# An output layernorm with a known mean: the rows of W2 and b2 centred once, z's squares summed on ScalarE

## What is computed

```python
x = x + gnn(layernorm(x))
#   h_neigh = segment_sum(h[src], dst) / deg
#   h = normalize(relu(h @ W_self[l] + h_neigh @ W_neigh[l] + b[l])),  l = 0, 1, 2
xn = layer_norm(layernorm(x), ln_g, ln_b)
top_p, top_i = top_k(softmax(xn @ Wg), 2);  conf = top_p / sum(top_p)
h = gelu(xn @ W1 + b1)                      # 8 experts x 64
combined = sum of conf * (h_e @ W2[e] + b2[e]) over the two experts
x = x + layer_norm(layernorm(x) + combined, out_g, out_b)
```

## Time and profile before

| what | value |
|---|---|
| median of three runs | 2080.27 us |
| the profiled execution | 2078.15 us, span 2076.4 us |
| granted TensorE clock over the span | 0.991 |
| TensorE busy | 1957.9 us (94%) |
| VectorE busy | 1627.2 us (78%) |
| ScalarE busy | 1034.4 us (50%) |
| GpSimd busy | 1225.1 us (59%) |

### The profile page before, as it was taken

How to read it: one execution, slowest core, us unless ns; L and a number is a source line. 1 busy time by engine, 2 the same in 40 slices (tenths; PEclk the granted TensorE clock), 3 DMA queues, 4 the chain that set the end, 5 groups by cost and what they waited for, 6 DMA issues and landing times.

```text
span 2076.4 us, 41132 instructions
## 1 busy us (share of the span) xinstructions
PE 1957.9 (94%) x13965; PEld 1064.1 (51%) x13965; DVE 1627.2 (78%) x3951; ACT 1034.4 (50%) x1877; POOL 1225.1 (59%) x1239
## 2 busy tenths in 40 slices
PE   6999999997999999999999999999899999999996
PEld 2444444443444444444444444444467767677774
DVE  7677986665777777776777777775689999999985
ACT  4444333332334434343344444553677777777762
POOL 2785116674656665664444444454568888888854
PEclk9999999998999999999999999999999999999998
DMA  6877678974787878874788886555878888878863
GB/s 209 205 184 230 238 253 151 142 136 119 189 192 202 193 196 188 202 187 147 207 236 233 235 233 191 175 172 165 224 171 180 183 186 186 182 179 181 185 99 50
DMA packets 330680, 384.93 MB, mean 185 GB/s; under 512 B 200057, under 2 KB 200231, under 8 KB 330471
## 3 DMA queue, kind: packets, MB, share of 16 engines
q1 hardware_dynamic: 269655, 216.86, 43.1%
q0 software_dynamic: 60816, 165.43, 31.1%
HBM read 175.81 MB, written 165.31 MB: 164 GB/s over the span
## 4 chain that ended last, share of the span: by engine, by line
PE 41%; DVE 25%; issue 12%; ACT 9%; DMA 8%; POOL 4%; SPq 0%; DVEq 0%; ACTq 0%; POOLq 0%
PE psY L578 18%; PE psS L578 18%; DMA w_n<-HH 6%; DVE R L1485 4%; ACT RR L1013 2%; POOL node_info L769 2%; DVE w_s L1693 2%; DVE area L1473 2%; DVE HH L1509 2%; DVE area L1683 2%; DVE st6b L1670 2%; PE psT L1798 2%; DVE w_s L1658 2%; DVE HH L1590 2%; DVE G L1473 1%
## 5 line engine op out<-in xcount | busy, mean ns | idle before, releaser
L578 PE MATMUL psY<-w_n,HT 128*128 128x512 f16 x1620 | 378.8, 384 | 21.8 <-DVE HT L1357 12.7
L578 PE MATMUL psS<-w_s,HT 128*128 128x512 f16 x1620 | 371.7, 379 | 0.0
L1013 ACT ACTIVATE RR<-R 128x512 f32<-128x512 f32 x237 | 149.6, 631 | 312.8 <-DVE R L1485 312.7
L878 POOL DMA_INDIRECT y_rows<-YB,poutT x158 | 160.8, 1018 | 198.0 <-DVE YB L1364 161.6
L578 PEld LDWEIGHTS psY<-w_n,HT 128*128 128x128 f16 x1620 | 157.5, 99 | 224.5 <-DVE HT L1357 23.9
L578 PEld LDWEIGHTS psS<-w_s,HT 128*128 128x128 f16 x1620 | 154.4, 98 | 167.8
L1374 DVE SCALAR_TENSOR_TENSOR SB<-psS,downs,bias 128x512 f32<-128x512 f32 x237 | 177.6, 749 | 76.6 <-PE psS L578 74.5
L578 PE MATMUL psY<-w_n 128*128 128x512 f16 x960 | 220.5, 379 | 12.4 <-DMA w_n<-HH 12.2
L578 PE MATMUL psS<-w_s,w_n 128*128 128x512 f16 x960 | 220.3, 379 | 0.0
L578 PE MATMUL psS<-w_w,w_s 128*128 128x512 f16 x948 | 217.5, 379 | 0.8 <-ACT w_s L1108 0.8
L1364 DVE SCALAR_TENSOR_TENSOR YB<-psY,YB 128x512 f16<-128x512 f32 x237 | 162.4, 685 | 47.8 <-ACT YB L980 47.6
(11 more groups left out here) (328 smaller groups left out, 3895.9 us busy)
## 6 DMA issues: line engine op xcount, KB each, us to landing
self_rows<-SB SPq DMA_DIRECT2D x236, 256.0 KB, 2.5
Sl<-self_rows SPq DMA_DIRECT2D x158, 256.0 KB
area<-in_x_dram SPq DMA_DIRECT2D x78, 256.0 KB, 5.1
y_rows<-YB SPq DMA_DIRECT2D x78, 256.0 KB, 5.1
out_dram<-obb SPq DMA_DIRECT2D x78, 256.0 KB
raw<-in_L_gnn_W_neigh_dram SPq DMA_DIRECT2D x12, 256.0 KB, 3.6
raw<-in_L_gnn_W_self_dram SPq DMA_DIRECT2D x12, 256.0 KB, 4.2
y_rows<-YB,poutT POOLq DMA_INDIRECT x158
```

The costliest lines, as they stand in the source:

```text
L578: mm = eng.matmul(acc, lhs[:, a, c, :], w[:, bpart, c, :], start=(c == 0 and n == 0), stop=(stop and c == KC - 1 and n == 2))
L878: pool.indirect_dma_start(Yd[l][:, :], bass.IndirectOffsetOnAxis(ap=poutT[:, t.t:t.t + 1], axis=0), YB[i][:, :], None, bounds_check=node_l ...
L1013: act.activation(RR[i][:, :], R[i][:, :], ACT.Relu).then_inc(s.rr, 1)
```

## The change

The rows of W2 (one per expert and hidden unit) and of b2 are centred: each row's mean is taken off. Then combined has mean 0 in every row, and z's mean is that of the residual part, a constant in the kernel's scale, `small[:, 7:8]`. z_gain subtracts this constant and waits for down alone. ScalarE sums the squares of z less the constant (z_squares), VectorE adds epsilon to one column (z_var), GpSimd takes the power as before. bn_stats and bn_aggr of z are gone. w2's steps move two later (WSTEP 24) and three jobs are new ahead of them.

```diff
 def WSTEP(m):
...
-    return 2 + 4 * (m - N_FIRST) + (m == 6)
+    return 2 + 4 * (m - N_FIRST) + (m >= 6) + (m == 7)
...
-            run_tiles(T, [(7, gather), (5, by_node), (4, norm3), (3, pow_of_group), (-10, zr_of),
-                          (-11, put_out)], 2)
+            run_tiles(T, [(7, gather), (-11, zr_of), (5, by_node), (4, norm3), (3, pow_of_group), (-11, put_out)], 2)
...
+                if name == "w2":
+                    act.wait_ge(s_wcent, 2)
                 after(act, s_cn, m)
                 act.activation(sqw, raw[:, m % 2, :, :], ACT.Square).then_inc(s_sq, 1)
...
-            def z_eps(t):
...
-                act.wait_ge(f3.aggz, (t + 1).n)
-                after(act, f3.zr, (t + -1).n)
-                act.activation(zv[:, i:i + 1], zm[:, i, 1:2], ACT.Identity, bias=ezb[:, t.group % 4, t.place:t.place + 1]
-                               ).then_inc(f3.zv, 1)
+            def z_squares(t):
...
+                act.wait_ge(f3.o1, (t + 1).n)
+                after(act, f3.zv, (t + -1).n)
+                act.activation(junk[:, :], psO[i][:, :], ACT.Square, bias=zshift[:, 0:1], scale=D ** -0.5,
+                               accum_out=zq[:, i:i + 1]).then_inc(f3.zq, 1)
...
+            def center_bias2():
+                rows = 6 * EXPERTS
+                dve.wait_ge(s_bload, 16 * 15)
+                link(dve.tensor_reduce(small[0:rows, 12:13], b2r[:, :], AX.X, ALU.add))
+                link(dve.tensor_scalar(small[0:rows, 12:13], small[0:rows, 12:13], -1.0 / D, None, ALU.mult))
+                dve.tensor_scalar(b2r[:, :], b2r[:, :], small[0:rows, 12:13], None, ALU.add).then_inc(s_wcent, 1)
+            def row_means():
+                m = C["w2"]
+                dve.wait_ge(s_wload[m % 2], 64 * (m // 2 + 1))
+                link(dve.tensor_reduce(small[:, 8:12], raw[:, m % 2, :, :], AX.X, ALU.add))
+                link(dve.tensor_scalar(small[:, 8:12], small[:, 8:12], -1.0 / D, None, ALU.mult))
+            def center_rows():
+                w = raw[:, C["w2"] % 2, :, :]
+                for c in range(KC):
+                    k = dve.tensor_scalar(w[:, c, :], w[:, c, :], small[:, 8 + c:9 + c], None, ALU.add)
+                k.then_inc(s_wcent, 1)
...
+                link(dve.tensor_scalar(zshift[:, :], small[:, 7:8], -(D ** -0.5), None, ALU.mult))
...
+                        (WSTEP(C["w2"]) - 3, center_bias2, None), (WSTEP(C["w2"]) - 2, row_means, None),
+                        (WSTEP(C["w2"]) - 1, center_rows, None),
...
-            def z_stats(t):
...
-                dve.bn_stats(st6b[:, :], psO[t.slot(2)][:, :]).then_inc(f3.bnz, 1)
-            def z_mean_var(t):
...
-                dve.bn_aggr(zm[:, t.slot(2), :], st6b[:, :]).then_inc(f3.aggz, 1)
+            def z_var(t):
...
+                dve.wait_ge(f3.zq, (t + 1).n)
+                after(dve, f3.zr, (t + -1).n)
+                dve.tensor_tensor(zv[:, i:i + 1], zq[:, i:i + 1], ezb[:, t.group % 4, t.place:t.place + 1], ALU.add
+                                  ).then_inc(f3.zv, 1)
             def z_gain(t):
...
-                dve.wait_ge(f3.aggz, (t + 1).n)
-                dve.scalar_tensor_tensor(Z[i], psO[i][:, :], zm[:, i, 0:1], ogb[:, :], ALU.subtract, ALU.mult
+                dve.wait_ge(f3.down, (t + 1).n)
+                dve.scalar_tensor_tensor(Z[i], psO[i][:, :], small[:, 7:8], ogb[:, :], ALU.subtract, ALU.mult
                                          ).then_inc(f3.o1, 1)
...
-            run_plan(T, [(-9, hs), (-5, confidences), (4, lambda t: carry_lo(t, 3)), (4, lambda t: combine(t, 3)), (3,
-                          x2), (-4, logits), (-9, flo), (4, norm_floor), (2, group_scales), (-4, largest), (-4, largest_index), (-4, gaps), (3, group_vars), (-10, z_stats), (-4, hots),
-                          (-10, z_mean_var), (-11, result), (-10, z_gain), (-1, xlo)],
+            run_plan(T, [(-9, hs), (-11, z_var), (-5, confidences), (4, lambda t: carry_lo(t, 3)), (4, lambda t: combine(t, 3)), (3,
+                          x2), (-4, logits), (-9, flo), (4, norm_floor), (2, group_scales), (-4, largest), (-4, largest_index), (-4, gaps), (3, group_vars), (-4, hots),
+                          (-11, result), (-10, z_gain), (-1, xlo)],
...
             def down(t):
...
-                after(pe, f3.o1, (t + -1).n)
+                after(pe, f3.zq, (t + -1).n)
```

More of the change, by code:

```diff
@@ L280, in __init__ @@
         self.down = sem("f3_down")
-        self.bnz = sem("f3_bnz")
-        self.aggz = sem("f3_aggz")
+        self.zq = sem("f3_zq")
         self.zv = sem("f3_zv")
@@ L419, in build @@
         s_wgain = sem("s_wgain")
+        s_wcent = sem("s_wcent")
         s_epad = sem("s_epad")
@@ L564, in build @@
         zv = sb("zv", [P, 2])
-        zm = sb("zm", [P, 2, 2])
-        st6b = sb("st6b", [P, 6])
+        zq = sb("zq", [P, 2])
+        zshift = sb("zshift", [P, 1])
         psA3 = [psA[0][:, :], psT[0].rearrange("p a c n -> p (a c n)").bitcast(F32)]
@@ L1110, in _ @@
             run_tiles(T, [(4, lambda t: carry_hi(t, 3)), (-9, fhi), (4, lambda t: relu(t, 3)), (4, sum_squares3), (-8,
-                          weights_in), (3, x2_deviations), (-1, xn), (-1, xhi), (-10, z_eps), (-4, gate_tanh), (-4, gelu)], 2)
+                          weights_in), (3, x2_deviations), (-1, xn), (-1, xhi), (-10, z_squares), (-4, gate_tanh), (-4, gelu)], 2)
         @block.vector
@@ L1665, in flo @@
                 dve.tensor_tensor(FH[i][:, 1, :], HS[i], FH[i][:, 0, :], ALU.subtract).then_inc(f3.flo, 1)
-            def z_stats(t):
+            def z_var(t):
                 t = t.own
-                dve.wait_ge(f3.down, (t + 1).n)
-                dve.bn_stats(st6b[:, :], psO[t.slot(2)][:, :]).then_inc(f3.bnz, 1)
-            def z_mean_var(t):
-                t = t.own
-                dve.wait_ge(f3.bnz, (t + 1).n)
-                after(dve, f3.zv, (t + -1).n)
-                dve.bn_aggr(zm[:, t.slot(2), :], st6b[:, :]).then_inc(f3.aggz, 1)
+                i = t.slot(2)
+                dve.wait_ge(f3.zq, (t + 1).n)
+                after(dve, f3.zr, (t + -1).n)
+                dve.tensor_tensor(zv[:, i:i + 1], zq[:, i:i + 1], ezb[:, t.group % 4, t.place:t.place + 1], ALU.add
+                                  ).then_inc(f3.zv, 1)
             def z_gain(t):
```

## The result

The changed kernel takes 2091.8 us (median of six runs, 2088.79 to 2096.39) beside 2077.74 for the kernel before (six runs): ratio 1.0076, interval 1.0059 to 1.0092. It is slower by 0.8%; forecast was 2075.5 us, between 2062 and 2086. It came out where the rival "GpSimd sets the pace" had put it (2091 us, chance 0.10); how far that was luck is said behind the experiments. The profiled execution took 2094.96 us (span 2093.2).

A forecast was written before the change was run, and what follows sets the result against it. The prediction took VectorE to bound the kernel's layer-3 part, at 28.99 us per four steps. From 2078.15 us it took 5.9 (steady part) and 1.5 (drain) and added 4.8 (first stage): 2075.5 us, range 2062 to 2086.

The forecast's parts named there:

- GpSimd sets the pace: Rival, layer 3 steady part: result waits for zr if GpSimd is late; 7.40 a step gives 2091 us; chance 0.10.
- GpSimd's order: Layer 3: zr_of moves from the step's end to behind the gather; costed at nothing, covered by GpSimd's slack.
- passes with two SBUF inputs stay four a step: Layer 3 steady part: argument against the GpSimd rival; result, x2, xlo and flo remain the contending VectorE passes.
- VectorE is rid of 0.73 a step: Layer 3 steady part: 0.83 us goes, z_var adds 0.10; VectorE's sum falls from 28.99 to 26.1 per four steps.
- The square costs 0.70 on the loop: Layer 3, ScalarE, combine to combine: 28.61 against 28.99 us per four steps, -5.9 us in all.
- What is late next: Layer 3 steady part: the next limit is ScalarE's chain, at 7.15 us a step, not TensorE.
- The drain: Last steps, without layer-3 tiles: 0.3 us saved in each of five steps, -1.5 us; ends 0 and -3.5.
- The first stage costs 4.8: First stage, w2: +2.54 row_means, +1.3 square sums, -1.35 wait gone, +2.34 weight_lo; ends 0 and +6.2.
- The sum: Whole kernel: 2078.15 - 5.9 - 1.5 + 4.8 = 2075.5 us.

The follow-up runs named there:

- The blocks: Five kernels, each run once: the kernel before plus a block behind its last step, GpSimd powers and gathers beside different VectorE work; no kernel time given.
- f3: Changed kernel with the power for zr ahead of the gather in GpSimd's order; 2074.76 us, ratio 0.9996 to the kernel before.
- f1: Changed kernel with result and put_out one step later, GpSimd's order kept; 2075.83 us, ratio 0.9989 to the kernel before.
- f2: f1 with the power for zr moved to the end of GpSimd's step; 2075.44 us, ratio 1.0006 to the kernel before.
- f6: Changed kernel with square ahead of relu and z_gain, z_var behind norm_floor, zr at GpSimd's step end, result one step later; 2063.45 us, ratio 0.9939.
- s1: Kernel before with only the centring and the shifted first-stage steps, z's statistics kept; 2081.89 us, ratio 1.0029.
- s2: Changed kernel without centring and with w2's steps where they were before; 2085.05 us, ratio 1.0034 to the kernel before.
- s3: Kernel before with only w2's first-stage steps later, nothing centred; 2079.22 us beside 2074.55, ratio 1.0021.

## Why the prediction was wrong

**The step that failed** is "GpSimd's order", the term for zr_of's move: "I cost the move at nothing; the cover is GpSimd's slack". The place where zr is made has no cover. The rows that would have said so are not among those of the prediction: GpSimd's timeline of the kernel before, here in the third step.

```profile
1809.29 2.12 POOL L922 DMA_INDIRECT out_dram<-w_s,poutT  x1 [0.18 <-issue]
1811.72 1.77 POOL L846 DMA_INDIRECT G<-y_rows,srcT  x1 [0.31 <-issue]
...
1815.71 0.54 POOL L913 TENSOR_TENSOR zr<-zv,halfpow 128x1 f32<-128x1 f32 x1
```

The gather ends at 1813.49, 2.43 after combine (1811.06), and so it does in the second and the fourth step (1806.23 and 1820.10). A power of 0.54 behind it ends 3.0 after combine. VectorE reaches result's place 3.20 and 3.26 after combine in the first two steps, but 2.60 and 2.67 in the third and fourth: against these places the power is 0.3 us early in the second step, and 0.4 and 0.3 late in the third and fourth. The prediction wanted the gather and the power done in the 3.2 us behind z_var, but gave neither a price and left put_out, here 2.12, out of them. In the changed kernel result waits for zr in the fourth and the second step, which are longer than forecast by 0.67 and 0.52; in the third its gather starts ahead of combine (1825.55, 1.05 long) and the power is just in time. The move also put a power under x2 and flo, out of a place at the step's end where it took 0.54 to 0.58 (median 543 ns of 59 from 1570 to 1990 us; 1132 ns of 57 in the changed kernel). The gathers of the kernel before were long already (up to 1.80, median 1.78 and 1.71 by buffer, where 1.04 is the least); the sign of this was in the trace as well.

By the numbers of the rival: GpSimd's work was 373.61 us in 62.1 steps (450 by 28.99 / 4), 6.02 a step, and is 403.88 in 60.5, 6.68 a step. The growth is 0.66; the rival had set 0.33 as the point from which it decides, and 0.48 as 2091 us. It overlooked 0.19 a step (11.9 us in all) in which GpSimd waited for zv and which goes too, so 0.52 was the slack, and 7.25 + 0.14 = 7.39 the pace; measured 7.44. That the rival's 7.40 is so near is luck: its growth was too small by 0.18 and its slack by 0.19. The argument against it ("passes with two SBUF inputs stay four a step") was about how many there are, and what changed is what of GpSimd's stands beside them. The Trainium skill ("GPSIMD Engine Reference", Specifications) names contention with VectorE's instructions with two SBUF inputs. The blocks agree for powers (three in 1.58 beside bn_stats and beside passes with a PSUM input, in 1.75 to 2.26 beside passes with two SBUF inputs) and in part for gathers (1.55 beside flo's form, 1.05 beside x2's); the sizes are from the runs alone.

**Point by point.**
- *VectorE is rid of 0.73 a step*: less, as far as busy time shows it. 431.66 in 62.1 steps and 389.59 in 60.5 is 6.95 and 6.44 a step, so 0.51 of busy time (result lasts up to 0.81 where it was 0.75, z_var 0.15 where 0.10 was taken). It decided nothing, since VectorE was no bound any more.
- *The square costs 0.70 on the loop, and the loop is 28.61*: right, but of a kernel without the wait for zr: 7.10 and 6.73 in the two transitions that have none, and 28.70 in f3. From the first combine of pass 3 to the last f3 is 4.35 us shorter than the kernel before (537.24 and 541.59), forecast was 5.9. Its time, 2074.8 us, is near the 2075.5 that was forecast, but as a ratio the forecast was 0.9987 and f1, f2 and f3 have 0.9989, 1.0006 and 0.9996, all near 1: so the sum is met within what the runs can tell, and only the trace shows the gain. What is late next was named rightly too, and f6 shows it: with the square off the loop the pace is TensorE's.
- *The drain*: right in this execution, -1.3 (forecast -1.5); z_gain comes every 4.07 there (2064.67 to 2068.74; 4.21 before), now held up by TensorE:

```profile
2064.67 0.75 DVE L1703 SCALAR_TENSOR_TENSOR area<-psS,small,ogb 128x512 f32<-128x512 f32 x1 [0.39 <-PE psS L1948]
...
2068.74 0.75 DVE L1703 SCALAR_TENSOR_TENSOR area<-psS,small,ogb 128x512 f32<-128x512 f32 x1 [0.39 <-PE psS L1948]
```

- *The first stage costs 4.8*: not refuted. The parts came (2.50 to 3.90 behind row_means, where 2.54 was forecast, the 1.35 at 188 gone, 2.19 at 217 behind weight_lo), in the changed kernel 5.8 in sum at TensorE's row at 220; part of it is the clock's fall behind the longest new wait, 1.4, which the prediction didn't have, and some 2 us more came at the stage's end. In the executions of the changed kernel, s1, f1, f2, f3 and f6, which share this stage, layer 1 starts 3.5 (f3) to 8.0 us late, and pass 3 0.5 (f3) to 8.2 (f2), but s2 and s3, which lack all or most of it, have pass 3 1.6 late and 2.7 early: one trace doesn't measure this. The ratio of s1, 1.0029, is some 6 us, with 3.5 to 8.7 in its interval.
- *The sum*: 2078.15 + 11.4 - 1.3 + 6.7 = 2094.95, the profiled execution's own time. These terms are read from the same two traces, so that they add up is no test; beside the forecast they say where it went wrong: 11.4 for -5.9, with -1.3 for -1.5 and 6.7 for 4.8.

## What to carry to other kernels

When an operation moves on an engine that "has slack", look at the place and not at the share: what stands ahead of it there, when that ends, and how long before its consumer; here one entry of a list decided 17 us. An engine whose instructions are stretched by a neighbour has no fixed load, so its slack in the trace of before can't be carried over. Work taken from the full engine pays only if it doesn't come back on the same loop at another engine: the square had to go in front of relu before the change brought more than 0.1%.

## What the hardware showed beside this

- GpSimd's small power zr took a median of 0.54 us at the end of the step (before and f2, 1570 to 1990 us), 1.13 behind the gather (changed kernel) and 2.29, up to 2.83, ahead of it (f3, with what its record shares with put_out's); an indirect gather 1.04 to 2.76 us. Busy time of GpSimd in 450 us ranged from 351.76 (f2) to 404.22 (the changed kernel) with the same instructions, by their order and by what stands beside them.
- A wait of 3.90 us of TensorE cost 1.4 us more in the twelve products behind it, their granted clock being 0.65. Behind waits of one length it went either way: of 2.19 and 2.18 with products of 2.76 (changed kernel, 217) and 4.42 (f6, 217); of 2.80 with 4.27 (before, 248) and 2.76 (s3, 251). By these rows one or two such stretches make single executions of this stage differ by some 1.4 to 3 us, an estimate.
